# Attention rows turned on VectorE, values product in 32x64 tiles of the array, and scores behind an FFN quarter

## The chip, the cores and the metric

The kernel runs on one core of a Trainium2 chip, as one launch. The metric is the device time in microseconds. Before the change it is 1148.92 us, the median of three runs (1147.48 to 1149.34). The core's engines run their own queues in order and meet through semaphores: TensorE (PE, matrix products, its weight loads are listed as PEld), VectorE (DVE), ScalarE (ACT), GpSimd (POOL), and SyncE (SP), which here issues the DMA transfers.

## The reference, cut to what matters

A decoder layer on x of 32 sequences x 64 tokens x 256, all in float32: first a gated delta-rule attention over the tokens (8 heads of 128), then a cross attention with compressed keys and values, then a gated FFN with integer weights; after each, a residual sum and a layer norm. The change lies in the cross attention:

```python
kv_c = kv @ W_kvc                                   # 64 numbers a token
q_nope, q_rope = (q_c @ W_uq), rope(q_c @ W_qr)     # 16 heads
k_nope, v = (kv_c @ W_uk), (kv_c @ W_uv)
scores = (q_nope . k_nope + q_rope . rope(kv_c @ W_kr)) * scale
good = (k_ids <= seg_id) & (k_ids >= seg_id - LOOKBACK)
attn = softmax(where(good, scores, NEG))            # 64 keys of the own sequence
out = (attn @ v) @ W_o
x = layernorm(x + out)
```

The kernel multiplies the weights together ahead (`w_qn` from W_uq and W_uk, `w_uvo` from W_uv and W_o), so for one tile it computes the scores against `kE` and `kO`, the softmax, the product of the attention rows with the compressed tokens `kvtok` (64 numbers a token), and the product of that with `w_uvo`.

## The kernel before

There are two phases. `delta_phase` computes the delta-rule attention in 32 units over slots. `tile_phase` takes its output in 16 tiles of 128 tokens (two sequences each) through output projection, cross attention and FFN. Some tile work is done ahead, in the last slots of the first phase: `out` of tiles 0, 1, 2, rope and nope of tiles 0 and 1, the scores and the softmax of tile 0.

The tile phase is a software pipeline. Step s of each engine's `loop` (s from 2 to 19) works on tile u1 = s (output projection, norm 0, rope and nope queries), u2 = s-1 (scores, softmax), u3 = s-2 (values product, cross result, norm 1), u4 = s-3 (FFN) and u5 = s-4 (norm 2, store). The order inside a step is written out by hand for each engine, and each engine goes through it in order. On TensorE (L1797 to L1867) it is: `out(u1)` 8 products, `scores(u2)` 32 products, two transposes of x2 (L1812), eight transposes of the attention rows (L1818), `turn_x1(u1)`, `ffn(0)`, `down_q`, `ffn(1)`, `rope`, `nope`, the values product (L1841), `ffn(2)`, `ffn(3)`, the cross product (L1854) and the down product (L1866). Each float32 product appears in the trace as two instructions (two passes), a transpose as one.

The scores of a tile lie as rows (h2, query) x columns (pair of heads, sequence, key) in `att`: `score_bank(u)[b]` holds sequence b, its partitions 0 to 63 are the queries for the even head of a pair and 64 to 127 those for the odd one. TensorE transposes these rows in eight 128x128 blocks into two PSUM banks, ScalarE copies them to `attT` (L1932), and the values product takes, for each sequence b and head half h2, a 64x64 piece of the array: weights `kvtok` of the sequence (64 tokens x 64), moving 512 columns (8 head pairs x 64 queries), output in bank b1 or b2. ScalarE copies that to `ctxT` (L1942).

On VectorE (L2064 to L2099) a step is: norm 2 of u5, norm 0 of u1, `mask_scores` and `softmax_max` of u2, `hidden(0)` and `hidden(1)` of u4, `rope_parts(u1)`, in steps 2 and 3 the unpacking of `w_up` and `w_down`, `hidden(2)`, `hidden(3)`, `softmax_sum(u2)`, norm 1 of u3, `good_keys(u1)`, which builds the mask of a tile. ScalarE's step (L1907 to L1952) holds the copies out of PSUM, the silu of the FFN quarters, the exp of the softmax and the norms' Ln and Exp, with two table loads a step.

SP loads `kvtok` once, in slot U+3 of the first phase (L422, a straight 512 KB copy of the scratch). After the last slot it loads tile 3's inputs (`load(3)`) and runs `weights_after_chain` (L424), which waits until the first phase has left the region "chain" and loads `w_uvo`, the integers of `w_up` and those of `w_down`. In each step `rope_rows` (L1690) issues 16 small transfers that put the rotated q into `qE` and `qO`, which the scores of the next step need.

## Time and profile before

| | |
|---|---|
| median of three runs | 1148.92 us |
| the profiled execution | span 1150.4 us |
| TensorE busy | 1101.5 us, 96% |
| its weight loads | 763.6 us, 66% |
| VectorE busy | 818.0 us, 71% |
| ScalarE busy | 707.8 us, 62% |
| GpSimd busy | 472.0 us, 41% |
| steps 4 to 15 of the tile phase | 782.15 to 1096.67 us |

How to read it: the span is that of the one execution that the profiler took. Busy times are over the whole span, in which the first phase takes some two thirds; the change lies in the last third, so its stages are to be read by themselves. A matmul's duration in the trace is longer than the distance to the next one, since they are pipelined: what an instruction costs TensorE is the distance from its start to the start of what follows.

### The profile page before, as it was taken

What the parts mean: (1) busy time and instruction counts of PE and PEld (TensorE: products, weight loads), DVE (VectorE), ACT (ScalarE), POOL (GpSimd) and SP (SyncE); (2) the same over time, 40 slices, a digit from 0 to 9 for tenths busy, and PEclk for the clock granted to TensorE, in tenths of its full rate; (3) what the DMA queues carried; (4) which work ended last, traced back from release to release, by engine and by line L of the source; (5) the groups of instructions that cost most, each with busy time, mean ns of one, the idle gap of its engine ahead of it and who ended that gap; (6) DMA issues with size and microseconds to landing.
All of it is one profiled execution on the core that took longest, in us unless ns stands there. A gap on an engine that the chain in (4) does not pass through costs nothing.

```text
span 1150.4 us, 28703 instructions
## 1 busy us (share of the span) xinstructions
PE 1101.5 (96%) x11420; PEld 763.6 (66%) x11420; DVE 818.0 (71%) x1429; ACT 707.8 (62%) x1243; POOL 472.0 (41%) x688
## 2 busy tenths in 40 slices
PE   8989799999999999999998899899999999999998
PEld 3444455555555555655554566679998999989987
DVE  5989769879779779779776756665666665655562
ACT  5777577687786777778676666554444444444433
POOL 1649484683882873964856512310000000110000
PEclk9999899999999999999998899999999999999999
DMA  4223345656565665666646332432222211112100
GB/s 131 56 63 88 86 73 86 132 106 101 126 94 110 124 115 96 133 138 143 141 88 219 103 121 66 134 95 51 51 53 67 51 48 47 47 48 50 29 19 10
DMA packets 164213, 101.82 MB, mean 89 GB/s; under 512 B 94289, under 2 KB 144593, under 8 KB 163185
## 3 DMA queue, kind: packets, MB, share of 16 engines
q1 hardware_dynamic: 162928, 99.78, 39.2%
q8 instruction: 91, 1.49, 0.6%
q14 instruction: 42, 0.34, 0.1%
q10 hardware_dynamic: 1152, 0.21, 0.1%
HBM read 62.72 MB, written 14.67 MB: 67 GB/s over the span
## 4 chain that ended last, share of the span: by engine, by line
PE 60%; DVE 12%; POOL 10%; issue 8%; ACT 4%; SPq 3%; DMA 3%; ACTq 0%; POOLq 0%; DVEq 0%
PE proj L581 13%; PE out L1792 5%; DVE conv L1213 5%; PE turned_v_chain L1792 5%; PE proj L1854 4%; PE turned_v_chain L1866 4%; PE proj L1731 4%; POOL inverse L1490 3%; POOL rank_one L1487 3%; PE gram L596 3%; PE gram L1766 2%; PE proj L1780 1%; PE turned_v_chain L587 1%; PE proj L1841 1%; PE out L605 1%
## 5 line engine op out<-in xcount | busy, mean ns | idle before, releaser
L1213 DVE SCALAR_TENSOR_TENSOR conv<-proj,kq_weights,conv 128x504 f32<-128x504 f32 (+2 forms) x261 | 189.7, 729 | 66.3 <-ACT conv L920 60.6
L581 PE MATMUL proj<-xT,vg_weights 128*128 128x512 f32 x384 | 194.1, 629 | 3.5 <-DMA vg_weights<-in_vg_w 2.2
L2109 POOL TENSOR_TENSOR rope<-rope_part,rope_part 128x512 f32<-128x512 f32 x32 | 42.1, 1336 | 321.5 <-DVE rope_part L2040 321.5
L581 PE MATMUL proj<-xT,kq_weights 128*128 128x512 f32 x348 | 167.7, 607 | 1.3 <-DVE conv L1213 1.0
L1213 DVE SCALAR_TENSOR_TENSOR conv<-proj,vg_weights,conv 128x504 f32<-128x504 f32 (+2 forms) x192 | 139.6, 728 | 26.4 <-ACT conv L920 23.3
L1490 POOL TENSOR_TENSOR inverse<-inverse,rank_one 128x30 f32<-128x30 f32 (+14 forms) x240 | 134.5, 560 | 18.8
L1487 POOL TENSOR_TENSOR rank_one<-inverse 128x30 f32<-128x30 f32 (+14 forms) x240 | 118.1, 492 | 22.9 <-DVE inverse L1274 8.0
L581 PEld LDWEIGHTS proj<-xT,kq_weights 128*128 128x128 f32 x348 | 62.4, 190 | 76.5 <-issue 64.0
L581 PEld LDWEIGHTS proj<-xT,vg_weights 128*128 128x128 f32 x384 | 66.9, 193 | 57.9 <-issue 50.0
L596 PEld LDWEIGHTS gram<-keys_q 128*64 128x64 f32 x896 | 56.8, 136 | 42.5 <-issue 24.9
L920 ACT ACTIVATE conv<-proj,kq_weights 128x512 f32<-128x512 f32 x87 | 59.6, 685 | 40.7 <-PE proj L581 40.3
L1875 ACT ACTIVATE rstd<-rstd 128x1 f32<-128x1 f32 x48 | 9.7, 202 | 121.8 <-DVE rstd L1987 121.8
L931 ACT ACTIVATE keys_q<-conv 128x512 f32<-128x512 f32 x96 | 63.5, 664 | 27.6 <-DVE conv L1213 26.9
L596 PE MATMUL gram<-keys_q 128*64 128x128 f32 (+2 forms) x896 | 73.4, 293 | 0.6 <-DVE kq_decayed L1244 0.6
L920 ACT ACTIVATE conv<-proj,vg_weights 128x512 f32<-128x512 f32 x64 | 43.9, 685 | 27.6 <-PE proj L581 27.3
L1854 PE MATMUL proj<-t_w_uvo,ctxT 128*128 128x256 f32 x256 | 58.0, 379 | 1.3 <-issue 1.3
L1587 POOL TENSOR_TENSOR W_scaled<-W,k_norm 128x512 f32<-128x512 f32 x32 | 34.9, 1090 | 57.6 <-ACT W L1040 57.6
L1866 PE MATMUL turned_v_chain<-t_w_down,hid 128*128 128x256 f32 x256 | 57.9, 379 | 0.0
L931 ACT ACT_TABLE_LOAD x41 | 52.6, 1283 | 6.2 <-DVE conv L1213 5.5
L1866 PEld LDWEIGHTS turned_v_chain<-t_w_down,hid 128*128 128x128 f32 x256 | 48.6, 190 | 6.6
L1596 POOL TENSOR_TENSOR o_sum<-o_sum,q_sq 128x512 f32<-128x512 f32 x23 | 29.4, 1279 | 57.2 <-ACT o_sum L1143 57.2
L1854 PEld LDWEIGHTS proj<-t_w_uvo,ctxT 128*128 128x128 f32 x256 | 47.4, 190 | 7.9 <-issue 2.1
(274 smaller groups left out, 2390.3 us busy)
## 6 DMA issues: line engine op xcount, KB each, us to landing
kq_weights<-in_kq_w SPq DMA_DIRECT2D x32, 390.0 KB, 6.5
vg_weights<-in_vg_w SPq DMA_DIRECT2D x32, 390.0 KB, 6.8
o_scratch<-oT SPq DMA_DIRECT2D x32, 256.0 KB, 2.2
o_in<-o_scratch SPq DMA_DIRECT2D x16, 512.0 KB, 4.1
o_rs<-o_rs_quarters SPq DMA_DIRECT2D x88, 64.0 KB, 6.1
diagonal<-gram_decayed SPq DMA_DIRECT2D x128, 32.0 KB, 2.0
inverse<-inverse SPq DMA_DIRECT2D x32, 128.0 KB, 2.8
q_first<-rope SPq DMA_DIRECT2D x128, 32.0 KB, 1.9
```

What stands on the lines that cost most here:

```text
L581: mm = e.matmul(bank(c, u)[:], w[:, (k * 3 + c % 3) * 128:(k * 3 + c % 3 + 1) * 128], xT[g][:, k, :], start=(k == 0), stop=(k == KD - 1))
L596: mm = e.matmul(out[p, b % 4, cols], kq[:, b, S:][:, p], kq[:, b, cols], start=True, stop=True)
L920: e.activation(acc(c, u)[:], bank(c, u)[:].rearrange("p (b l) -> p b l", l=S), ACT.Copy, scale=weights(c, u)[:, j:j + 1]).then_inc(s_tap[c ...
L931: e.activation(out, acc(c, u)[:], ACT.Silu).then_inc(s_silu[c], 1)
L1213: e.scalar_tensor_tensor(acc(c, u)[:, :, back:], src[:, :, 0:S - back], weights(c, u)[:, j:j + 1], acc(c, u)[:, :, back:], ALU.mult, ALU.a ...
L1487: e.tensor_tensor(product, X[:, k + 1:, k:k + 1].broadcast_to([128, n, k]), X[:, k:k + 1, 0:k].broadcast_to([128, n, k]), ALU.mult).then_i ...
L1490: e.tensor_tensor(X[:, k + 1:, 0:k], X[:, k + 1:, 0:k], product, ALU.add).then_inc(s_elim, 1)
L1731: mm = e.matmul(out_bank(u)[:, 0:D], o_in[u % 2][:, h, :], w_out[:, h, :], start=(h == 0), stop=(h == H - 1))
L1792: mm = e.matmul(ffn_bank[r][:, (2 * i + j) * TILE:(2 * i + j + 1) * TILE], wt[:, k, (2 * r + j) * 128:(2 * r + j + 1) * 128], x2T[:, k, :] ...
L1854: mm = e.matmul(b0[:, 0:D], ctxT[:, hp].rearrange("p b q -> p (b q)"), w_uvo[:, hp, :], start=(hp == 0), stop=(hp == XH // 2 - 1))
L1866: mm = e.matmul(b6[:, 0:D], hid[:, k, :], w_down[:, k, :], start=(k == 0), stop=(k == FJ - 1))
L2109: e.tensor_tensor(turned[half][:].rearrange("p b r q -> p r b q"), parts[2 * half][:], parts[2 * half + 1][:], op).then_inc(s_turned, 1)
```

## The change

Four things change together.

1. The attention rows are laid out as (sequence, query) x (head, key): `att` is [128, 16, 64], `score_bank(u)[half]` holds eight heads, and partitions 0 to 63 are sequence 0, 64 to 127 sequence 1. The mask becomes one row of 64 keys for each partition ([128, 64] instead of [128, 2, 64]), and `seg` has a column for each tile.
2. TensorE's eight transposes and ScalarE's two copies are gone. Instead VectorE does one `transpose` of the 128x1024 attention rows (`turn_att`), which turns each 32x32 block in its place, at the end of its step, for the tile whose softmax it has just finished. `turn_att(0)` stands ahead of the loop.
3. The values product (`mix`) works with 32 keys at a time: for key half k, partition group i of 32 and head parity h2, 16 products in 32x64 tiles of the array, 256 columns each, into four banks (one for each i). Its weights `kvtok` are laid out anew, 32 partitions x (tile, key half, 64), twice the size. They are loaded in `weights_after_chain`, by four transfers, ahead of `w_uvo`. ScalarE copies the four banks to `ctxT`.
4. The order of the steps changes. TensorE: `out(u1)`, x2 transposes, `mix(u3)`, `ffn(0)`, `scores(u2)`, `turn_x1`, `ffn(1)`, `down_q`, `ffn(2)`, `rope`, `nope`, `ffn(3)`, cross, down. VectorE: norms 2 and 0, `hidden(0)`, `mask_scores`, `softmax_max`, `hidden(1)`, unpacking, `hidden(2)`, `rope_parts`, `good_keys`, `hidden(3)`, `softmax_sum`, norm 1, `turn_att(u2)`. ScalarE: x2T copy, norm 2, the ctx copies, norm 0, silu 0, x1 copy, silu 1, q copy, silu 2, the nope copies, silu 3, table, exp, norm 1.

The core of the diff:

```diff
                 def weights_after_chain():
                     e.wait_ge(s_proj[G], U)
+                    for i in range(4):
+                        e.dma_start(tiles["kvtok"][32 * i:32 * i + 32],
+                                    scratch["kvtok"][64 * (i // 2):64 * (i // 2) + 64].rearrange("(k p) n c -> p n k c", p=32)).then_inc(d_kvtok, 16)
                     e.dma_start(tiles["w_uvo"][:], scratch["w_uvo"]).then_inc(d_uvo, 16)
...
+        mix_bank = (b1, b2, b3, b4)
+        turned_att = attT[:].rearrange("p (h c) (k q) -> p h c k q", c=2, k=2)
...
                 def scores(u):
-                    wait(e, s_ctx, 2 * (u - 1))
-                    for b in range(2):
-                        for hp in range(XH // 2):
-                            q, k = (qE, kE) if hp < 4 else (qO, kO)
-                            for h2 in range(2):
-                                mm = e.matmul(score_bank(u)[b][64 * h2:64 * h2 + 64, hp * S:(hp + 1) * S], q[:, b, 2 * hp % 8 + h2, :],
+                    wait(e, s_mask, 2 * u)
+                    wait(e, s_ctx, 4 * u - 2)
+                    for half, (q, k) in enumerate(((qE, kE), (qO, kO))):
+                        for h in range(XH // 2):
+                            for b in range(2):
+                                mm = e.matmul(score_bank(u)[half][64 * b:64 * b + 64, h * S:(h + 1) * S], q[:, b, h, :],
                                               k[:, u * TILE + b * S:u * TILE + (b + 1) * S], start=True, stop=True)
...
+                def mix(u):
+                    if u == 0:
+                        e.wait_ge(done["kvtok"], 64)
+                    e.wait_ge(s_attT, u + 1)
+                    wait(e, s_nopeout, 4 * (u + 2) if live(u + 1) else 0)
+                    wait(e, s_mask, 2 * (u + 1))
+                    wait(e, s_ctx, 4 * u)
+                    for k in range(2):
+                        for i in range(4):
+                            row = slice(32 * i, 32 * i + 32)
+                            for h2 in range(2):
+                                mm = e.matmul(mix_bank[i][64 * h2:64 * h2 + 64, 0:256], kvtok[row, u, k, :],
+                                              turned_att[row, :, h2, k, :], start=(k == 0), stop=(k == 1))
+                    mm.then_inc(s_mix, 1)
...
-                            for hp in range(XH // 2):
-                                mm = e.transpose((b3, b4)[hp // 4][:, (hp % 4) * 128:(hp % 4 + 1) * 128],
-                                                 att[u3 % 2][:, hp].rearrange("p b k -> p (b k)"), ident[:])
-                            mm.then_inc(s_attT, 1)
...
+                            for i, bk in enumerate(mix_bank):
+                                e.activation(ctxT[:, :, i // 2, i % 2 * 32:(i % 2 + 1) * 32],
+                                             bk[:, 0:256].rearrange("p (h q) -> p h q", h=XH // 2), ACT.Copy).then_inc(s_ctx, 1)
...
+                def turn_att(u):
+                    if u == 0:
+                        e.wait_ge(done["scaled"], U)
+                    e.wait_ge(s_soft, 5 * (u + 1))
+                    wait(e, s_mix, u)
+                    e.transpose(attT[:].rearrange("p h k -> p (h k)"), att[u % 2][:].rearrange("p h k -> p (h k)")).then_inc(s_attT, 1)
```

## Rows read from the trace of the kernel before

**Rows 1.** The page, granted TensorE clock and busy digits in 40 slices

```profile
PE   8989799999999999999998899899999999999998
...
PEclk9999899999999999999998899999999999999999
```

**Rows 2.** Windows: busy us of PE, PEld, DVE, ACT, POOL; granted clock, DMA

```profile
900.00:950.00 50.00, 50.00 (x444) 44.96 (x444) 31.24 (x67) 23.08 (x47) 5.00 (x4) 1.00 0.22 54
```

**Rows 3.** Timeline of TensorE, one step: start, us, engine, line, operation, operands

```profile
913.20 3.62 PE L1731 MATMUL proj<-t_w_out,o_in 128*128 128x256 f32 x16
916.75 0.69 PE L1780 MATMUL proj<-t_kE,q_first 128*64 128x64 f32 x16
...
918.76 0.44 PE L1812 MATMUL turned_v_chain<-ident,x 128*128 128x128 f32 x2
919.04 1.04 PE L1818 MATMUL gram<-ident,att 128*128 128x128 f32 x8
919.91 0.38 PE L1740 MATMUL turned_v_chain<-ident,x 128*128 128x128 f32 x2
...
925.93 1.95 PE L1766 MATMUL gram<-qc,t_w_qn 96*128 96x128 f32 x16
927.81 0.65 PE L1841 MATMUL proj<-attT,kvtok 64*64 64x512 f32 x2
...
928.29 0.60 PE L1841 MATMUL proj<-attT,kvtok 64*64 64x512 f32 x2
...
928.83 1.16 PE L1792 MATMUL out<-x2T,t_w_gate 128*128 128x128 f32 x8
...
932.50 3.62 PE L1854 MATMUL proj<-t_w_uvo,ctxT 128*128 128x256 f32 x16
...
939.41 0.81 PE L1731 MATMUL proj<-t_w_out,o_in 128*128 128x256 f32 x3
```

**Rows 4.** Timeline of ScalarE and VectorE, around the softmax of a step

```profile
906.49 0.38 ACT L1904 ACTIVATE gact<-turned_v_chain 128x256 f32<-128x256 f32 x1 [0.96 <-PE turned_v_chain L1792]
...
908.19 1.06 ACT L1899 ACTIVATE att<-att 128x1024 f32<-128x1024 f32 x1
909.27 1.22 DVE L2029 TENSOR_REDUCE total<-att 128x16 f32<-128x1024 f32 x1 [1.95 <-ACT att L1899]
...
911.96 0.42 DVE L1980 TENSOR_TENSOR res<-proj,x 128x256 f32<-128x256 f32 x1
...
914.07 0.29 DVE L1969 TENSOR_TENSOR mask<-t_keys,seg 128x128 f32<-128x128 f32 x1
...
930.38 0.60 ACT L1942 ACTIVATE ctxT<-proj 128x512 f32<-128x512 f32 x1
```

**Rows 5.** Groups by line and form, VectorE: busy us, mean ns, idle before

```profile
L1287 DVE STREAM_TRANSPOSE inverse<-inverse 128x1024 f32<-128x1024 f32 x8 | 16.7, 2092 | 2.1 <-POOL inverse L1570 2.0
L1291 DVE STREAM_TRANSPOSE inverse_turned<-inverse 128x1024 f32<-128x1024 f32 x8 | 15.5, 1942 | 0.0
```

**Rows 6.** Start of the phase: timeline, and DMA issues (KB, us to landing)

```profile
739.91 0.32 SPq L429 DMA_DIRECT2D t_w_uvo<-w_uvo_scratch  x1
...
t_w_uvo<-w_uvo_scratch SPq DMA_DIRECT2D x1, 1024.0 KB, 6.3
...
t_w_qn<-w_qn_scratch SPq DMA_DIRECT2D x2, 192.0 KB, 3.5
...
744.60 0.68 DVE L2015 SCALAR_TENSOR_TENSOR att<-proj,mask 128x512 f32<-128x512 f32 x1
...
748.80 2.36 DVE L2055 SCALAR_TENSOR_TENSOR t_w_up<-w_up_ints,w_up_scale 128x1024 f32<-128x1024 int32 x2 [0.41 <-DMA w_up_ints<-in_up_w]
...
782.15 3.62 PE L1731 MATMUL proj<-t_w_out,o_in 128*128 128x256 f32 x16
```

**Rows 7.** Timeline of TensorE at the end of the phase

```profile
1093.22 3.62 PE L1866 MATMUL turned_v_chain<-t_w_down,hid 128*128 128x256 f32 x16
1098.42 0.69 PE L1780 MATMUL proj<-t_kE,q_first 128*64 128x64 f32 x16 [1.58 <-DMA q_second<-rope]
...
1134.29 0.38 PE L1812 MATMUL turned_v_chain<-ident,x 128*128 128x128 f32 x2
```

More of the change, by code:

```diff
@@ L225, in delta_phase @@
         tiles["w_uvo"] = room.again("chain", "t_w_uvo", [128, XH // 2, D])
+        tiles["kvtok"] = room.again("chain", "kvtok", [128, NT, 2, KVC])
         tiles["x_in"] = [room.again("prepare", f"x_in{i}", [128, D]) for i in range(2)]
-        tiles["kvtok"] = room.again("prepare", "kvtok", [128, NT, KVC])
         scales = {n: room.again(region, f"{n}_scale", [128, k]) for n, k, region in (
@@ L421, in first_tiles @@
                         e.dma_start(tiles["x_in"][i][:], a["x"][i * TILE:(i + 1) * TILE, :]).then_inc(d_first, 16)
-                    e.dma_start(tiles["kvtok"][:], scratch["kvtok"]).then_inc(d_w, 16)
                 def weights_after_chain():
@@ L1616, in delta_phase @@
     tiles["ints"], tiles["scales"] = ints, scales
-    done = {"o": s_og, "w_high": s_whiout, "scaled": s_gr, "stored": d_out, "weights": d_w, "first": d_first, "uvo": d_uvo, "ffn": s_wgt, "up": d_up, "down": d_down, "scales": d_gate,
+    done = {"o": s_og, "w_high": s_whiout, "scaled": s_gr, "stored": d_out, "weights": d_w, "kvtok": d_kvtok, "first": d_first, "uvo": d_uvo, "ffn": s_wgt, "up": d_up, "down": d_down, "scales": d_gate,
             "gram": s_gm, "gate": s_silu[G], "v1": s_conv[V1], "high": s_wlo, "low": s_wloout, "solve": s_solve}
@@ L1634, in tile_phase @@
         place = (early, t, t)
-        seg, below = early("seg", [128, B]), early("below", [128, 2, S])
-        mask = [early(f"mask{i}", [128, 2, S]) for i in range(2)]
+        seg, below = early("seg", [128, NT]), early("below", [128, S])
+        mask = [early(f"mask{i}", [128, S]) for i in range(2)]
         x1 = [early(f"x1_{i}", [128, D]) for i in range(3)]
@@ L1827, in loop @@
                             ffn(0, u4)
+                        if live(u2):
+                            scores(u2)
+                        if live(u1) and u1 > AHEAD:
+                            turn_x1(u1)
+                        if live(u4):
+                            ffn(1, u4)
                         if live(u1) and u1 > AHEAD:
@@ L1830, in loop @@
                         if live(u4):
-                            ffn(1, u4)
+                            ffn(2, u4)
                         if live(u1):
@@ L1835, in loop @@
                             nope(u1)
-                        if live(u3):
-                            e.wait_ge(s_attout, 2 * (u3 + 1))
-                            wait(e, s_mask, 2 * (u3 + 2) if live(u3 + 1) else 0)
-                            for b in range(2):
-                                for h2 in range(2):
-                                    mm = e.matmul((b1, b2)[b][64 * h2:64 * h2 + 64, :], kvtok[64 * b:64 * b + 64, u3, :],
-                                                  attT[64 * b:64 * b + 64, :, h2, :], start=True, stop=True)
-                            mm.then_inc(s_mix, 1)
                         if live(u4):
-                            ffn(2, u4)
                             ffn(3, u4)
@@ L1917, in loop @@
                             e.activation(x2T[:], b5[:, 0:KD * TILE].rearrange("p (k n) -> p k n", k=KD), ACT.Copy).then_inc(s_x2tout, 1)
-                        if live(u5) and not live(u1):
+                        if live(u5):
                             rsqrt(2, u5)
+                        if live(u3):
+                            e.wait_ge(s_mix, u3 + 1)
+                            wait(e, s_cross, u3)
+                            for i, bk in enumerate(mix_bank):
+                                e.activation(ctxT[:, :, i // 2, i % 2 * 32:(i % 2 + 1) * 32],
+                                             bk[:, 0:256].rearrange("p (h q) -> p h q", h=XH // 2), ACT.Copy).then_inc(s_ctx, 1)
+                        if live(u1) and u1 > AHEAD:
+                            rsqrt(0, u1)
+                        if live(u4):
+                            silu(0, u4)
                         if live(u1) and u1 > AHEAD:
@@ L2065, in loop @@
                     e.wait_ge(done["o"], U)
+                    turn_att(0)
                     for s in span:
@@ L2073, in loop @@
                             normalize(0, u1)
+                        if live(u4):
+                            hidden(0, u4)
                         if live(u2):
@@ L2077, in loop @@
                         if live(u4):
-                            hidden(0, u4)
                             hidden(1, u4)
-                        if live(u1) and u1 > AHEAD:
-                            rope_parts(u1)
                         if s == AHEAD:
@@ L2087, in loop @@
                             hidden(2, u4)
+                        if live(u1) and u1 > AHEAD:
+                            rope_parts(u1)
+                        if live(u1):
+                            good_keys(u1)
+                        if live(u4):
                             hidden(3, u4)
```

81 lines of the change are left out of this document (25 added, 56 removed).

## The prediction

> **What bounds the kernel now.** I read the page first. TensorE's busy digits are 8 and 9 all through the span and its granted clock is full in the second part [rows 1]. The change touches only the tile phase, so I then took the windows of that phase: from 900 to 950 us TensorE is busy 50.00 of 50 us at clock 1.00, VectorE 31.24, ScalarE 23.08 [rows 2]. There each tile costs what TensorE's instructions cost, and anything taken off its queue is gained, as long as no other chain gets longer than TensorE's own turn. Third, the timeline of one step gives that turn: first `out` at 913.20, next at 939.41, so 26.21 us [rows 3]. Fourth, the same timeline on ScalarE and VectorE gives the one chain that the change lengthens [rows 4]. The edges of the phase, where TensorE does wait, I read last [rows 6, 7].
>
> **TensorE's queue.** Removed: eight transposes of the attention rows, 919.04 to 919.91 = 0.87 us a tile [rows 3]. Scores move behind an FFN quarter and keep their 32 products; only the pairing changes (the two columns of the array now hold two sequences instead of two heads). The number of changes between 128x128 and smaller tiles of the array stays: mix and scores each still stand between full-size work. The x1 transposes move but cost the same.
> The values product changes from 4 matmuls of 64x64 with 512 columns to 16 of 32x64 with 256 columns. Before, all four ran at once: the first passes start at 927.81, the second at 928.29, and the next FFN quarter at 928.83, so 1.02 us in all, of which 2 x 0.48 is streaming [rows 3]. A pass of 256 columns is half as long, each of the eight tiles has four of them: 4 x 0.24 = 0.96, plus the same ending, about 1.02 again, if all eight tiles run at once. No row shows eight, or a tile of 32 rows next to three others. Bounds: below, the streaming can't shrink (each tile streams as many columns as before), so 0.96; above, if the row groups took turns (only the two column halves together), 4 x 0.96 = 3.8 us. I take 1.05, because the four-tile rows start within 0.01 us of each other with the same feeding of rows by partition and, as now, one bank for each row group.
> So a turn is 26.21 - 0.87 + 0.03 = 25.37 us.
>
> **VectorE's and ScalarE's queues.** Added: one stream transpose of 128x1024 a tile. The rows nearest are the two of the same size in the first phase, 1942 and 2092 ns [rows 5]; their access is strided, the new one's isn't. The 1942 row reads straight and writes strided; I take 1.95. Below, it can't beat the 1.22 us that the plain 1024-element operations take [rows 4]. ScalarE loses two 512-column copies and has the two ctx copies cut in four. Neither engine is full [rows 2], so only order counts. What is queued behind the new wait: `turn_att` is last in VectorE's step, behind the norm of the cross result, and `sums(2)` and `sums(0)` of the next step stand behind it; TensorE waits for it in `mix`.
> The chain starts at nope's end on TensorE, which comes a turn less one FFN quarter (half of 3.67) and cross and down (6.91) after `out` starts, at 16.65 [rows 3]. Four q copies, 2.57 (927.81 to 930.38); silu and table load 1.70 (906.49 to 908.19); exp 1.08; softmax sum, reciprocal, product 2.69 (909.27 to 911.96); the norm 2.11 (911.96 to 914.07); the transpose 1.95 and 0.05 to hand over [rows 4, 5]. Sum 12.15, so the turned rows are there at 28.8, which is 3.45 in the next step, and 3.6 with some 0.1 for hand-overs that these rows don't show. TensorE reaches `mix` after `out` with the change of tiles (3.55) and two transposes (0.28 at most), at 3.8 [rows 3]. So the transpose is hidden, with 0.2 us of cover; without that cover each further us costs one us in every step. SP's 16 row copies for the rotated q start from rope's end, which is nope's start, 13.5 before a step ends (925.93 to 939.41); where the scores waited for them, they came at 1098.42, 1.75 into the step, 15.2 after rope [rows 3, 7]. Now nope starts 10.6 before the step ends and the scores 6.8 into the next, 17.4 apart, so these copies stay hidden. The masks are half as wide (they start at 914.07 [rows 4]), hidden like before.
>
> **The start of the phase** (steps 2 and 3). kvtok was loaded long before and was free. Now it is loaded twice as large (1 MB) in pieces of 256 bytes, after the last wait of the first phase, ahead of w_uvo, w_up and w_down, and `mix(0)` with scores(1) and everything behind it waits for it. Its first issue takes w_uvo's place at 739.91. If it were as fast as w_uvo (6.3 us) it would land at 746.2; by the other 256-byte load, 384 KB in two issues 0.6 apart with 3.5 to landing (4.1 us, of which I count 1.9 as fixed, an estimate), 1 MB moves in 5.9 and with w_uvo's queueing lands near 750 [rows 6]. I take 747.4. w_uvo, w_up and w_down land some 4 us later, still ahead of their use. Then: mix(0) to 748.4; scores(1) wait for two ctx copies, from 749.4 to 751.4; mask and maximum 3.8 (744.60 to 748.39) to 755.4; unpacking w_up 2.36 to 757.8; masks 0.8 (an estimate: four operations of at most 0.29, overlapping [rows 4]); the norm 2.2 to 760.8; softmax sum 2.7 to 763.5; the transpose to 765.5 [rows 6]. From `mix(1)` the rest of step 3 takes a turn less 3.8: `out(4)` starts at 787.1 instead of 782.15 [rows 6]. **Loss: 4.95 us.**
>
> **The steady steps** 4 to 15: 12 x (26.21 - 25.37) = **10.1 us gained.**
>
> **The end.** Step 16 begins where the last full product of step 15 ends, 1093.22 + 3.45 = 1096.67; before, x2 of the last tile was turned at 1134.29, 37.6 later [rows 7]. New: `mix(14)` still waits for the chain, at 3.6, though no `out` fills the time; ffn(0) (with its first product 1.9) and the scores (2.0 and the change of tiles) end at 8.6 [rows 3]; mask and maximum to 12.6; `hidden(1)`, which VectorE now does behind them, to 13.1, and ffn(3) waits for it; silu and table 16.8; exp 17.9; sum 20.6; norm 22.7; the transpose 24.7. Then mix(15) and two FFN quarters, while VectorE and ScalarE do the delayed norm up to its scalar step (1.8 of the 2.11), four ctx copies (1.3, an estimate: cut in four, 0.5 to 0.6 each uncut before), table and silu 1.7, hidden 0.4 (as the 0.42 of the sum at 911.96), to 29.9 [rows 4]; two quarters 3.6, cross and down 6.9: 40.4. **Loss: 2.8 us.** What follows is as before.
>
> **Sum**: +4.95 - 10.1 + 2.8 = -2.3 us. On the profiled execution, 1150.4 to 1148.1. The median shown is 1.5 us below it; the same difference gives 1148.9 - 2.3 = **1146.6 us**.
>
> **The rivals.**
> A. *VectorE's transpose is as fast as its other 1024-element work*, 1.22 instead of 1.95, because it reads and writes straight. For: both rows of 2 us are strided. Against: the one with a straight read is hardly shorter. The steady step gains nothing (it is hidden), the start 0.7, the end twice 0.7 and the wait behind it, 1.8 in all: 1144.1. The Trainium skill (Vector Engine (DVE) Microarchitecture Reference, The reshape front-end and per-opcode configuration) says that the 32x32 transpose sustains one element per cycle and lane. By that rule this rival is the case; the 1942 and 2092 ns rows do not agree with it [rows 5].
> B. *The 32-row tiles don't all run together.* If four of eight do, mix is 2 x 0.96 + 0.1 = 2.0, 1.0 more in 16 tiles, and it lies on both TensorE's turn and the start's and end's chains: +15, 1162. The sign turns at 1.05 + 2.3/16 = 1.2 us for one tile's product. For: no row has it. Against: the four-tile rows lose nothing. The Trainium skill (TensorE: Matmul & The Clock Gate, Packing small matmuls) gives 3.07 of 4 for four row groups and 10.6 of 16 for sixteen tiles; an estimate at 70% of eight, with 32 passes of 0.216 (sixteen in 3.46 [rows 3]), is 6.9 / 5.6 = 1.2 us, where the change would be worth nothing; the trace has no such packing.
> C. *The chain on VectorE becomes the bound.* Its cover is 0.2 us. With the 2092 ns transpose and 0.1 more on two of the hand-overs, each of 12 steps waits 0.15, and start and end lose 0.2 to 0.4: 1149.
> D. *kvtok lands late*, near 750 or beyond because each issue writes 32 partitions only. Everything behind mix(0) moves by that: +2.6 to +4: 1149 to 1151.
>
> **How the numbers follow.** 0.2% of this kernel is 2.3 us, about what a measurement can tell from no change. The forecast has 0.38, its own range 1144.5 to 1148.5, half on each side of that bound (0.20 faster, 0.18 same). A 0.20, faster. B 0.18, slower. C 0.14: 0.10 same, 0.04 slower. D 0.10: 0.04 same, 0.06 slower. Together faster 0.40, same 0.32, slower 0.28. The range leaves out B's far part and reaches over A and D: 1142.5 to 1154.
>
> **What would show it.** Steady steps: `out` to `out` 25.4, TensorE without idle time before `mix`; if TensorE waits there for VectorE's transpose, C. The duration of the transpose decides A. The time from mix's first matmul to the next FFN quarter decides B. In the start: the landing of kvtok, and out(4) at 787. At the end: 40.4 us from step 16 to the last x2 transpose, with waits before mix(14), ffn(3) and mix(15). Wrong would be above all a steady turn that isn't 0.8 us shorter.

## The result and the profile after

| | before | after |
|---|---|---|
| median | 1148.19 us (1145.31 to 1150.19) | 1151.13 us (1149.09 to 1154.68) |
| ratio to before, 95% interval | 1 | 1.0027 (1.0017 to 1.0036) |
| profiled execution, span | 1150.4 us | 1146.9 us |

The kernel is 3.1 us slower (0.27% of 1148), where I forecast 2.3 us faster; the time lies inside the range of 1142.5 to 1154. The two spans have the opposite order of the two medians, so they mustn't be subtracted. An execution takes 2.2 us more than its span (1149.09 for 1146.9), so the span of 1150.4 belongs to an execution some 4 us slower than its kernel's median. In the second traces (e11, e12 below) the spans are 1144.7 and 1149.6. I therefore count every trace from a mark ahead of everything that the change touches in the tile phase: the first product of `rope(2)`.

The page of after: busy digits and granted clock of TensorE in 40 slices, to be held against [rows 1].

```profile
PE   8989899999999999999988899689999999999988
...
PEclk9999799999999999999999999989999999999999
```

The 26th slice (717 to 745 us) has a 6 where before has an 8. Windows of after (us; busy PE, PEld, DVE, ACT, POOL; granted clock; DMA share and GB/s), the second to be read beside [rows 2]:

```profile
700.00:750.00 50.00, 37.10 (x488) 26.50 (x488) 28.00 (x47) 23.15 (x43) 12.87 (x9) 0.92 0.44 120
900.00:950.00 50.00, 50.00 (x491) 45.56 (x490) 35.38 (x71) 21.76 (x48) 5.01 (x4) 1.00 0.21 54
```

In the middle TensorE is as full as before. At the start it idles 13 of 50 us. The timeline of TensorE in one steady step of after (start, us, engine, line, operation, operands):

```profile
914.28 3.64 PE L1733 MATMUL proj<-t_w_out,o_in 128*128 128x256 f32 x16
917.76 0.38 PE L1827 MATMUL turned_v_chain<-ident,x 128*128 128x128 f32 x2
918.07 0.43 PE L1810 MATMUL proj<-attT,kvtok 32*64 32x256 f32 x2
918.08 0.43 PE L1810 MATMUL decays<-attT,kvtok 32*64 32x256 f32 x2
918.10 0.45 PE L1810 MATMUL gram<-attT,kvtok 32*64 32x256 f32 x4
918.34 0.38 PE L1810 MATMUL proj<-attT,kvtok 32*64 32x256 f32 x2
...
919.12 1.16 PE L1794 MATMUL out<-x2T,t_w_gate 128*128 128x128 f32 x8
...
939.67 1.71 PE L1733 MATMUL proj<-t_w_out,o_in 128*128 128x256 f32 x7
```

From `out` to `out` 25.39 us, where [rows 3] have 26.21. The mix takes 1.05 us (918.07 to 919.12); its eight tiles start within 0.03 us of each other. There is no wait ahead of it. VectorE's transposes, by line and form (busy us, mean ns, idle before), beside [rows 5], and the one of this step:

```profile
L2033 DVE STREAM_TRANSPOSE attT<-att 128x1024 f32<-128x1024 f32 x16 | 19.8, 1238 | 0.0
L1289 DVE STREAM_TRANSPOSE inverse<-inverse 128x1024 f32<-128x1024 f32 x8 | 16.8, 2105 | 2.1 <-POOL inverse L1572 2.0
L1293 DVE STREAM_TRANSPOSE inverse_turned<-inverse 128x1024 f32<-128x1024 f32 x8 | 15.7, 1961 | 0.0
```

```profile
915.83 1.24 DVE L2033 STREAM_TRANSPOSE attT<-att 128x1024 f32<-128x1024 f32 x1
```

The same operation on as many elements takes 1238 ns read and written straight and 1961 or 2105 ns with strides. It ends at 917.07, 1.00 us ahead of the mix. Now the start of the phase in after: timeline of TensorE and of SP's queue (SPq), to be held against [rows 6].

```profile
735.38 1.16 PE L1759 MATMUL turned_v_chain<-qc,t_w_qr 96*128 96x128 f32 x8 [0.36 <-ACT qc L1892]
736.75 5.37 SPq L429 DMA_DIRECT2D kvtok<-kvtok_scratch  x4
742.16 1.22 SPq L431 DMA_DIRECT2D t_w_uvo<-w_uvo_scratch  x1
746.33 0.69 PE L1810 MATMUL proj<-attT,kvtok 32*64 32x256 f32 x2 [8.90 <-DMA kvtok<-kvtok_scratch]
...
749.25 1.98 PE L1782 MATMUL proj<-t_kE,q_first 128*64 128x64 f32 x32 [0.90 <-ACT ctxT L1925]
750.98 1.67 PE L1782 MATMUL decays<-t_kO,q_second 128*64 128x64 f32 x32
752.59 2.05 PE L1768 MATMUL gram<-qc,t_w_qn 96*128 96x128 f32 x16
...
787.30 3.65 PE L1733 MATMUL proj<-t_w_out,o_in 128*128 128x256 f32 x16
```

The same stretch in the chain of waits that ended last (start, us, what):

```profile
736.75 0.57 SPq L429
737.36 0.70 SPq L429
738.11 2.81 SPq L429
740.96 5.33 DMA kvtok<-kvtok_scratch
746.33 0.69 PE proj L1810 x2
...
756.41 2.35 DVE t_w_up L2055 x2
```

SP needs 5.37 us to issue the four pieces of kvtok. The fourth issue begins at 740.96, 4.21 us behind the first, and lands 5.33 us after it began. TensorE, whose queue has `mix(0)` next, stands still for 8.90 us. Behind the wait the products go at half speed: scores(1) take 3.3 us (749.25 to 752.59) where a steady step has 2.0. The granted clock of that stretch is 0.55, so for most of it TensorE has the lower of its two clock levels, 1.2 instead of 2.4 GHz (windows of after, columns as above):

```profile
745.00:753.00 8.00, 5.76 (x99) 4.61 (x100) 0.31 (x1) 1.21 (x4) 0.00 (x0) 0.55 1.01 379
```

The end, beside [rows 7]:

```profile
1093.74 0.44 PE L1827 MATMUL turned_v_chain<-ident,x 128*128 128x128 f32 x2 [1.53 <-DVE x L2001]
1094.89 0.43 PE L1810 MATMUL proj<-attT,kvtok 32*64 32x256 f32 x2 [0.72 <-DVE attT L2033]
...
1130.68 0.38 PE L1827 MATMUL turned_v_chain<-ident,x 128*128 128x128 f32 x2
```

Counted from rope(2), in us, with the second traces beside the first ones:

| stretch | before | before (e11) | after | after (e12) |
|---|---|---|---|---|
| rope(2) to out(4) | 42.05 | 42.05 | 51.92 | 52.20 |
| out(4) to the down product of step 15 | 311.06 | 311.06 | 301.29 | 301.30 |
| from there to the end of the span | 57.23 | 57.45 | 58.26 | 59.85 |
| rope(2) to the end | 410.34 | 410.56 | 411.47 | 413.35 |

So the change costs 9.9 to 10.1 us at the start, gains 9.8 in the steady steps and costs 1.0 to 2.4 at the end: +1.1 in the first trace of after, +2.8 in the second, against +3.1 measured by the ratio.

### The profile page after: what moved, and what is told of

Its sections match the earlier page's. It is cut to its first block, busy times and chain, and to the rows that moved or that the text cites. A ratio compares the mean times of both kernels' runs of the same rounds, so it can differ in the third digit from the quotient of the medians.

```text
span 1146.9 us, 29249 instructions
## 1 busy us (share of the span) xinstructions
PE 1086.5 (95%) x11676; PEld 754.1 (66%) x11676; DVE 847.6 (74%) x1445; ACT 693.9 (61%) x1243; POOL 471.7 (41%) x688
## 4 chain that ended last, share of the span: by engine, by line
PE 59%; DVE 14%; POOL 10%; issue 7%; ACT 4%; DMA 3%; SPq 3%; ACTq 0%; DVEq 0%; POOLq 0%
PE proj L583 13%; DVE conv L1215 5%; PE out L1794 5%; PE turned_v_chain L1794 5%; PE turned_v_chain L1871 4%; PE proj L1859 4%; PE proj L1733 4%; POOL inverse L1492 3%; PE gram L598 3%; POOL rank_one L1489 3%; PE gram L1768 2%; PE proj L1782 1%; DMA vg_weights<-in_vg_w 1%; PE turned_v_chain L589 1%; PE proj L1810 1%
## 5 line engine op out<-in xcount | busy, mean ns | idle before, releaser
L1733 PE MATMUL proj<-t_w_out,o_in 128*128 128x256 f32 x224 | 51.1, 381 | 1.9 <-issue 1.9
```

The costliest lines, as they stand in the source:

```text
L1733: mm = e.matmul(out_bank(u)[:, 0:D], o_in[u % 2][:, h, :], w_out[:, h, :], start=(h == 0), stop=(h == H - 1))
```

## The experiments

Theory W: the steady gain is real, and the start eats it, because mix(0) holds TensorE's queue for a load that is issued last and cut small, with the clock falling behind the wait. Rival O: the new order itself costs it, since scores(1) and everything that hangs on mask(1) now stand behind mix(0) and its copies. Rivals for a part of it: the cut of the load rather than its place, the clock, and VectorE's chain in the steady step. Each ratio is to executions of before taken alongside, whose medians lie between 1147.4 and 1149.3 us, so kernels are compared by their ratios rather than by their medians. e1 to e7 have 12 executions each, e8 has 5, e9 and e10 have 6. The last two columns come from one trace each.

| kernel | median | ratio (95%) | rope(2) to out(4) | rope(2) to end |
|---|---|---|---|---|
| after | 1151.13 | 1.0027 (1.0017 to 1.0036) | 51.92 | 411.5 |
| e1 kvtok early | 1144.96 | 0.9973 (0.9961 to 0.9985) | 46.70 | 406.3 |
| e2 busy wait | 1150.21 | 1.0027 (1.0016 to 1.0038) | 51.66 | 412.9 |
| e3 before, kvtok late | 1148.14 | 1.001 (0.9998 to 1.0021) | 43.22 | 411.6 |
| e4 mix(0) last | 1148.72 | 1.001 (0.9998 to 1.0021) | 48.82 | 410.0 |
| e5 both | 1145.07 | 0.9973 (0.996 to 0.9986) | 45.60 | 405.2 |
| e6 both, scores(15) first | 1148.81 | 1.0006 (0.9992 to 1.002) | 45.45 | 411.1 |
| e7 straight load | 1149.51 | 1.0018 (1.0004 to 1.0032) | 49.75 | 410.9 |
| e8 turned twice | 1161.95 | 1.012 (1.0099 to 1.0141) | 55.11 | 424.0 |
| e9 both, sum first | 1141.63 | 0.993 (0.9913 to 0.9947) | 43.84 | 405.0 |
| e10 as e9, end reordered | 1142.69 | 0.9946 (0.9927 to 0.9966) | 44.71 | 404.8 |

**e1, kvtok with the first tiles.** It takes the sbuf place of w_up's scale, which moves behind w_uvo.

```diff
     def first_tiles():
+        for i in range(4):
+            e.dma_start(tiles["kvtok"][32 * i:32 * i + 32], ...)
     def weights_after_chain():
-        for i in range(4):
-            e.dma_start(tiles["kvtok"][32 * i:32 * i + 32], ...)
         e.dma_start(tiles["w_uvo"][:], ...)
+        e.dma_start(scales["w_up"][:], a["up_scale"])
```

> The kernel after, with the four kvtok transfers issued with the first tiles' loads instead of behind the whole chain of the first phase (kvtok takes the place of w_up's scale in the sbuf, and that scale is loaded behind w_uvo). Everything is computed. Theory W (the late, finely cut kvtok load holds TensorE's queue): attT(0) ends at 741.10 in the trace of after, 3.7 us behind rope(2)'s end at 737.4, so the wait ahead of mix(0) falls from 8.90 to about 3.7 us and turns into one on VectorE; the halved clock behind it (mix(0) passes 0.43 instead of 0.21 us, scores(1) 3.3 instead of 2.0) goes too or gets shorter. 5.2 to 7.5 us less than after: 1143.6 to 1146 us, some 2 to 4.5 below before. Theory O (the new order costs at the start: scores(1) stands behind mix(0) and its four ScalarE copies, and everything later hangs on mask(1) and the chain behind it, whatever kvtok does): at most 2 us less than after, 1149 to 1151, not below before.

Theory W is borne out: 1144.96 us, and out(4) 5.2 us earlier. The load is gone from TensorE's waits (timeline of e1; its rope(2) began at 737.91):

```profile
743.73 0.69 PE L1811 MATMUL proj<-attT,kvtok 32*64 32x256 f32 x2 [3.77 <-issue]
...
746.64 1.97 PE L1783 MATMUL proj<-t_kE,q_first 128*64 128x64 f32 x32 [0.90 <-ACT ctxT L1926]
```

3.77 us are left, until attT(0) is there, and the clock still falls (0.54 from 743 to 750). This one edit turns the loss of 0.27% into a gain of 0.27%.

**e2, TensorE busy while it waits.**

```diff
 def mix(u):
+    if u == 0:
+        for _ in range(18):
+            e.matmul(b1[:, 0:256], ident[:], kE[:, 0:256], start=True, stop=True)
     if u == 0: e.wait_ge(done["kvtok"], 64)
```

(Not in this excerpt: mix's waits for banks and masks are moved ahead of the 18 products.)

> The kernel after, with 18 matmuls of 256 columns (identity by kE, into a bank that scores(1) overwrites) in front of the kvtok wait of mix(0), some 7.7 us at full clock: the wait stays, TensorE is busy through most of it. Everything of the kernel is computed. Theory W with the clock as its second part: kvtok still lands at about 746.3, but the granted clock does not fall behind it, so mix(0) takes 1.05 instead of about 1.9 us and scores(1) 2.0 instead of 3.3: about 2.2 us less than after, 1149 us. Rival (the half clock has no part in the loss, or the clock falls in any case): within 0.5 us of after, 1151.

By the ratio, nothing is gained. The trace shows a gain at the place itself that is lost later: nope(2) begins 15.2 us after rope(2) instead of 17.2, so 2.0 us are saved by full clock; then the first FFN quarter of step 3 runs at half speed, behind two waits of 1.9 us each, where after had full speed. The clock granted behind the wait is 1.00 here, against the 0.55 of after (window of e2):

```profile
745.00:750.00 5.00, 3.37 (x98) 2.81 (x99) 0.12 (x1) 1.21 (x4) 0.00 (x0) 1.00 1.02 403
```

```profile
745.73 0.43 PE L1812 MATMUL proj<-attT,kvtok 32*64 32x256 f32 x2 [1.35 <-DMA kvtok<-kvtok_scratch]
...
762.99 0.43 PE L1812 MATMUL proj<-attT,kvtok 32*64 32x256 f32 x2 [1.87 <-DVE attT L2035]
...
764.04 2.08 PE L1794 MATMUL out<-x2T,t_w_gate 128*128 128x128 f32 x8
```

In this trace the price of the clock was taken in another place, and by the ratio it could not be mended by itself.

**e3, the kernel before with its straight kvtok load at the late place.**

```diff
 def weights_after_chain():
+    e.dma_start(tiles["kvtok"][:], scratch["kvtok"])
     e.dma_start(tiles["w_uvo"][:], ...)
```

> The kernel before, its kvtok load left in one straight piece of 512 KB but moved to where the kernel after has it: behind the chain of the first phase, ahead of w_uvo. Everything is computed. If a late load by itself is harmless and the harm lies in the cut (four issues of 1024 short rows each, 5.37 us of SyncE and 5.3 to 6.9 us to land): one straight issue of some 0.4 us lands by about 743 to 745, at or before the time when the mix(0) of before comes up (its scores(1) are masked at 744.6), and the time is that of before within 1 us, 1148 us. If the place in the queue does the harm (kvtok's own landing, or w_uvo, w_up and w_down half a megabyte later): 3 us or more slower than before, 1151 or above.

One straight issue of 512 KB takes SP 0.32 us and lands in 5.2 us, at 741.5, and the mix of before comes up at 743.03 and doesn't wait. Only w_up's unpacking starts 2.4 us later, counted from rope(2), than in e11, and out(4) comes 1.2 us later: 1.001. So this load at the late place is nearly harmless for the old order: 1.2 us in the trace, and a ratio that can't be told from 1. It is half as large as after's and uncut, though. The mix of before comes up 8.3 us behind rope(2), and after's load lands 10.95 us behind it; from these two an estimate for the old order with after's load is a wait of 2.6 us. No run had it.

```profile
736.34 0.32 SPq L428 DMA_DIRECT2D kvtok<-kvtok_scratch  x1
...
750.87 3.69 PE L1731 MATMUL proj<-t_w_out,o_in 128*128 128x256 f32 x16 [1.80 <-issue]
```

**e4, the first mix behind scores(1) and nope(2).**

```diff
 if live(u3):
+    if u3 == 0:
+        scores(u2)
+        nope(u1)
     mix(u3)
```

> The kernel after, with only the first mix behind scores(1) and nope(2) in its step (and the ScalarE copies of mix(0) behind those of nope(2)); all other steps keep the order of the change. Everything is computed. Theory W (it is a block of TensorE's queue by a late load): the 3.8 us of scores(1) and nope(2) fill part of the 8.9 us wait, mask(1) comes at about 741 instead of 752.7, mix(0) still waits to 746.3, for about 5 us. From there the step has 3.8 us less to do, and scores(1) does not run at half clock: 4 to 6 us less than after, 1145 to 1147 us. Theory O agrees in sign, since the order is mended: it expects the whole 9.9 us of the start back, 1141 us, as the chain behind mask(1) is then 11.7 us earlier. Rival (loss in the steady steps or the end): no difference, 1151.

1148.7 us: about half of what theory W expected, a quarter of what O did. The wait is still 5.62 us, and now the cross product stands in the slow stretch (clock 0.61 from 746 to 757) and takes 5.86 us instead of 3.62:

```profile
746.77 0.69 PE L1810 MATMUL proj<-attT,kvtok 32*64 32x256 f32 x2 [5.62 <-DMA kvtok<-kvtok_scratch]
...
750.20 5.86 PE L1862 MATMUL proj<-t_w_uvo,ctxT 128*128 128x256 f32 x16 [1.42 <-issue]
```

**e5, both mends together.**

> The two mends together: the kernel after with kvtok loaded with the first tiles and, in its first step only, mix(0) behind scores(1) and nope(2). Everything is computed. Measured from the start of rope(2), out(4) came at 42.0 us in the trace of before, 51.9 in after, 46.7 with kvtok early, 48.8 with mix(0) last. In the last of these mix(0) still waited 5.6 us for kvtok, and mix(0) and the cross product ran at half clock for 3.2 us more. If the start's loss is this wait and the clock behind it, both go and out(4) comes at about 40 to 43 us, the median at 1139 to 1142 us, 6 to 9 below before (ratio 0.992 to 0.995). If the two mends get hold of the same microseconds (VectorE's chain with w_up's unpacking then sets attT(1)), out(4) stays at 45 to 46 and the time at 1144 to 1145, that of kvtok early.

By the numbers it is the second of the two cases: out(4) at 45.6, the time that of e1. The two mends get hold of the same microseconds. The reason is another than the expectation's, w_up's unpacking: the cross product runs at half speed here too, 6.43 us instead of 3.62, and VectorE waits for it ahead of softmax_sum(1), which e9 takes up. With kvtok there, mix(0) waits for something new: ScalarE's four copies of nope(2), whose banks it needs, and mix(1) waits for attT(1) as in after.

```profile
744.39 0.43 PE L1811 MATMUL proj<-attT,kvtok 32*64 32x256 f32 x2 [2.73 <-ACT q_second L1903]
...
746.92 6.43 PE L1863 MATMUL proj<-t_w_uvo,ctxT 128*128 128x256 f32 x16 [1.40 <-issue]
...
759.60 0.43 PE L1811 MATMUL proj<-attT,kvtok 32*64 32x256 f32 x2 [1.78 <-DVE attT L2039]
```

**e6, besides scores(15) at the head of step 16.**

```diff
+if u2 == NT - 1: scores(u2)
 (x2 transposes, ffn(0, u4))
+if u2 == NT - 1: mix(u3)
```

(Not in this excerpt: ScalarE's silu(0) of that step goes ahead of the ctx copies, and VectorE's mask(15) to the head of its step.)

> As the kernel with both mends, and besides in the first step without an output projection (step 16 of the tile phase) scores(15) ahead of the x2 transposes, mix(14) behind the first FFN quarter, ScalarE's silu(0) ahead of the copies of ctx and VectorE's mask(15) at the head of its step. Everything is computed. In after, the waits of that step and the next are 1.53 us for x2, 0.72 for attT(14), 0.47 for hid, 0.85 for x2 and 0.71 for attT(15). If these are what the new order costs at the end, scores(15) covers the first two and an earlier mask(15) the last: 1.5 to 3 us less than the kernel with both mends. If they are only moved (mix(14) waiting for mask(15), cross for the later copies): within 0.5 us of it.

Refuted, 3.7 us slower than e5. At the head of its step scores(15) waits for the last row copies of the rotated queries, 4.93 us, and half clock follows (its 32 products take 3.6 us instead of 2.0). Without `out` nothing else covers the copies, which the change's later place of the scores does. Since mix(14), silu(0) and mask(15) moved with them, how much of the 3.7 us is the scores' is not shown apart; the wait is 4.93.

```profile
1091.72 1.98 PE L1783 MATMUL proj<-t_kE,q_first 128*64 128x64 f32 x32 [4.93 <-DMA q_second<-rope]
```

**e7, the load straight, at the late place.** The scratch is written in the order of the tile (eight small stores for each of four large ones), and one issue reads 128 rows of 8 KB.

```diff
 def weights_after_chain():
-    for i in range(4):
-        e.dma_start(tiles["kvtok"][32 * i:32 * i + 32], scratch["kvtok"][...].rearrange("(k p) n c -> p n k c", p=32))
+    e.dma_start(tiles["kvtok"][:], scratch["kvtok"])
```

> The kernel after, its kvtok load at the same place but straight: the stores of the first phase write the scratch in the order of the tile (eight pieces for each of four, in place of one), and one issue reads 128 rows of 8 KB, the same 1 MB. Everything is computed. Theory C (the cut of the load is what is late: 5.37 us of issues on SyncE and the last piece landing 6.9 us after its own): one issue lands 6.3 us later, as w_uvo's 1 MB does, at about 743 where after has 746.3: the wait at mix(0) falls from 8.9 to about 5.5 us and w_uvo comes 5 us sooner; 3 to 4 us less than after, 1147 to 1148 us, level with before. Theory S (it is the size and the place): the wait stays over 8 us and the time within 1 us of after. The longer stores could cost something in the first phase; the start of rope(2) in the trace would show that.

The same 1 MB lands 7.0 us after its issue began, instead of 9.6; the wait falls from 8.90 to 6.44 us, and out(4) comes 2.2 us sooner. The ratio is 1.0018, 1 us below that of after with overlapping intervals, short of the 3 to 4 us expected (theory C had the wait at 5.5). So by the trace the cut has about a quarter of the start's 9.9 us; moving the load (e1) gives back 5.2.

```profile
744.74 0.69 PE L1811 MATMUL proj<-attT,kvtok 32*64 32x256 f32 x2 [6.44 <-DMA kvtok<-kvtok_scratch]
```

**e8, each tile's rows turned twice on VectorE.**

```diff
+e.transpose(attT, att[u % 2]).then_inc(s_twice, 1)
+e.wait_ge(s_twice, u + 1)
 e.transpose(attT, att[u % 2]).then_inc(s_attT, 1)
```

> The kernel after with VectorE turning each tile's attention rows twice, the second after the first. Everything is computed. In the steady step of after, attT is ready at 917.07 and TensorE comes to the mix at 918.04: 0.97 us of cover. A second transposition of 1.24 us with its hand-over moves attT by 1.3 us. If TensorE sets the step and this cover is all there is, each of the 12 steady steps gets 0.3 to 0.4 us longer (a wait on attT ahead of each mix, step 25.7 us) and the waits at start and end some 1.3 us each, 3 times: 8 us more than after, 1159 us. If VectorE's chain were already the bound of the step, the whole 1.3 us would show in each: 16 us and more, 1169 or above. If the cover is larger than the trace shows: within 3 us of after.

The steady step becomes 25.73 us (917.40 to 943.13), +0.34, with a wait of 0.26 ahead of the mix: of 1.25 us more on VectorE, 0.9 to 1.0 were hidden. The cover of 1.00 us that the trace shows is the cover there is, and TensorE sets the step. Of the 12.5 us that the trace has more than after's, 4.1 are these steps; the rest lies where there was no cover, 3.2 at the start and 5.3 from step 15's down product on, half clock there included, for which the expectation had too little (8 us in all).

```profile
917.40 3.64 PE L1733 MATMUL proj<-t_w_out,o_in 128*128 128x256 f32 x16
...
920.23 1.25 DVE L2035 STREAM_TRANSPOSE attT<-att 128x1024 f32<-128x1024 f32 x1
...
921.53 0.43 PE L1810 MATMUL proj<-attT,kvtok 32*64 32x256 f32 x2 [0.26 <-DVE attT L2035]
```

**e9, e5 with softmax_sum(1) at its usual place.**

```diff
-if live(u2) and u3 != 0: softmax_sum(u2)
+if live(u2): softmax_sum(u2)
 (sums(1, u3), normalize(1, u3))
-if u3 == 0: softmax_sum(u2)
```

> The kernel with both mends, and VectorE's softmax_sum(1) in the first step at the place that it has in all others, ahead of the residual sums of x2 instead of behind them. Everything is computed. In the trace of both mends exp(1) ends at 749.19 and VectorE then idles 3.18 us for the cross product, does the sums, and only then softmax_sum(1) and turn_att(1); mix(1) waits 1.78 us for attT(1). If that wait stands on the path to out(4), it goes: 1.5 to 1.8 us less than both mends, 1143.4 us, ratio to before 0.996. If something else takes its place (x2T, the fourth bank, SyncE's rope rows), within 0.5 us of both mends, 1145.

The wait of mix(1) is gone (its products start at 757.46 behind the x2 transposes, without one), and out(4) comes 1.76 us sooner than in e5. This is the version that beats both kernels: 1141.63 us, ratio 0.993 (0.9913 to 0.9947), some 8 us faster than before. More than the 0.996 expected, and clear of e5's interval (0.996 to 0.9986). In its trace half clock stood in step 16 as well, so that rope(2) to the end is only 0.2 us less than in e5. The cross product of its first step still takes 6.53 us instead of 3.62, at a clock of 0.56.

**e10, e9 with the last two steps rearranged** (x2's sums ahead of softmax_sum from step 15 on, mix(14) and mix(15) behind the first FFN quarter).

> The kernel of the run before it, and the last two steps rearranged: from step 15 on VectorE does the sums of x2 ahead of softmax_sum, and in steps 16 and 17 mix stands behind the first FFN quarter. Everything is computed. In after these two steps wait 1.53 and 0.85 us for x2 and 0.72 and 0.71 for attT, and both waits stand ahead of the first FFN quarter. If this is what the new order costs at the end, x2 comes before it is asked for and the FFN quarter covers attT: 2 to 3.5 us less than the kernel without it, 1140 to 1141.5 us, ratio 0.994, and less of the half clock that was seen near 1093 in four of the runs. If the waits only move (scores(15) for the copies of mix(14)): within 0.7 us of it. The earlier try at the end waited 4.93 us for the rope rows of step 15, which SyncE delivers at 0.6 us a piece; here scores(15) is not moved ahead.

Nothing gained, 0.9946 with overlapping intervals: the waits move. For x2 and attT TensorE no longer waits, but for these (waits of e10: us in total, times, longest):

```profile
PE out L1795 <- DVE hid L2056: 1.8, 1, 1.8
PE out L1795 <- ACT x2T L1925: 1.4, 3, 0.5
...
PE proj L1783 <- ACT ctxT L1934: 1.2, 1, 1.2
```

**e11 and e12, before and after once more, unchanged.**

> The kernel before, unchanged, for a second trace. In its first trace rope(2) began at 740.11 with the clock at half for 10.2, 6.8 and 3.4 us in the stretch from 600 to 740; in all nine traces of its variants and of after it began between 733.2 and 737.9. If that trace was a late one for reasons of the first phase only, this one has rope(2) at about 735 and the same 410.3 us from there to the end of the span (to within 0.5), so that the comparison of the tile phases stands: after is 1.1 us longer there. If the tile phase of before itself differs from one execution to the next, the 410.3 will not come back.

> The kernel after, unchanged, for a second trace. Its first trace had a mean granted clock of 0.986, the highest of its 17 runs (mean 0.983), and an execution time 2.0 us below its median. Four variants of it showed the clock at half for 3.4 us near 1093, where TensorE waits for x2 and attT in the first step without an output projection. If that is what the typical execution has and the first trace lacked, this trace shows it, with 1.7 us more from rope(2) to the end: 413 instead of 411.5 us. If not, the 2 us lie in the first phase.

Both as expected: before has 410.56 us from rope(2) to the end (410.34 in its first trace) and 42.05 to out(4), to the hundredth. After has 413.35: 0.3 us more at the start, and half clock in step 16 behind the waits for x2 and attT. In e12 the FFN quarter of 2.0 us takes 3.5 there:

```profile
1094.95 0.44 PE L1827 MATMUL turned_v_chain<-ident,x 128*128 128x128 f32 x2 [1.53 <-DVE x L2001]
...
1097.18 2.08 PE L1794 MATMUL out<-x2T,t_w_gate 128*128 128x128 f32 x8
1099.05 1.74 PE L1794 MATMUL out<-x2T,t_w_up 128*128 128x128 f32 x8
```

And e11 shows what was peculiar in the first trace of before: there w_uvo was issued 0.20 us ahead of rope(2), here 1.64 us behind it. TensorE's granted clock from 735 to 740 us was 0.67 there, and `rope(2)` began 11.63 us behind `out(2)` instead of 10.26. The trace of e9 has the same (0.68 from 730 to 735), and its w_uvo was issued 0.01 us ahead of rope(2). In the other twelve traces SP's first issue of these weights came 1.1 to 2.1 us behind it.

```profile
734.12 1.16 PE L1757 MATMUL turned_v_chain<-qc,t_w_qr 96*128 96x128 f32 x8 [0.36 <-ACT qc L1887]
...
735.76 0.32 SPq L429 DMA_DIRECT2D t_w_uvo<-w_uvo_scratch  x1
```

## Why the prediction was wrong

**TensorE's turn: right.** 25.37 forecast, 25.39 measured; the mix at 1.05 as taken, so rival B is out. The twelve steps brought 9.8 us instead of 10.1.

**VectorE's transpose: rival A.** 1.24 us, not 1.95. I let the strided rows of the first phase decide [rows 5] where the unstrided 1024-element rows [rows 4] were the nearer kin. The rule of the Trainium skill that was named there (Vector Engine (DVE) Microarchitecture Reference, The reshape front-end and per-opcode configuration: one element per cycle and lane) agrees with L2033, which is as fast as a plain operation of that size, and not with L1289 and L1293, which it doesn't tell apart. The chain is ready 0.8 us earlier than in my sum (0.7 of it the transpose's), the cover is 1.0 us instead of 0.2, and rival C is out (e8).

**The start: the step that failed.** 4.95 us of loss forecast, 9.87 in the first trace. By its terms, counted from rope(2):
- *When the load is issued.* I put it 0.20 us ahead of rope(2), from [rows 6]. It came 1.37 behind: **+1.6**. In that trace of before TensorE had half clock just ahead of rope(2), so that rope(2) was 1.4 us late against SP's queue; in e11 the same issue stands at +1.64. Two queues that don't wait for each other had been tied together by one execution.
- *How long it takes.* I took 7.5 us from the first issue to the landing (747.4 less 739.91); it was 9.6: **+2.1**. It is the cut, into four issues and short rows: e7's straight load needs 7.0. SP alone is busy 5.37 us with four issues; I had the row of two such issues 0.6 us apart and didn't carry it on to four issues of more rows.
- *The clock.* I had no term for it: **+2.0** (e2 gives it: nope(2) at 15.2 instead of 17.2; counted from the start of mix(0) it is 4.0 instead of 6.3, since e2's load landed 0.2 later). The window from 900 to 950 has clock 1.00, and I used durations at full clock behind a wait that I had forecast myself. The page of before already shows three 8s in its clock row, all of them in slices where TensorE's own row has a 7 or an 8, and two of them just past the middle of the span, where I had called the clock full [rows 1].
- *The transpose*, faster: **-0.7**.

Together 4.95 + 1.6 + 2.1 + 2.0 - 0.7 = 9.95. My sum also went from 751.4 by 3.8 to 755.4, 0.2 too far, and did the same at the end (8.6 to 12.6), too little to matter. Rival D (kvtok lands late, 1149 to 1151 us) had the right event, a late landing that moves everything behind mix(0), and its landing "near 750 or beyond" was right as well: 10.95 us behind rope(2) is 751.1 in the time of that trace. I gave it 0.10. Its reason, that each issue writes 32 partitions only, no run tested by itself, and that its time of 1149 to 1151 us was met is partly luck, since 1.4 of the 1.6 us by which the issue came late are TensorE's clock in one trace of before and the time holds the clock's 2.0 as well. The issue's place and the landing are 3.7 of the 5.0 us that the start was off, and the landing's part lies in choosing 747.4 nearer to the straight w_uvo than to the other load of 256-byte pieces, whose estimate was 750. The Trainium skill says of such loads (DMA: Bandwidth & Descriptors, Specifications) that below 512 bytes a piece they lose line rate; e7 against after agrees, 7.0 against 9.6 us for the same megabyte. But e7 has one issue instead of four as well, and after's fourth begins 4.21 us behind its first; no run here tells the short pieces from the time of the issues.

**The end: right in kind, too large.** From the start of step 16 to the last x2 transposes 38.6 us instead of 40.4, which is what rival A gives; the loss is 1.0 us in the first trace, not 2.8. In e12 half clock behind the waits of step 16 adds 1.6 (2.4 in all, against e11), so the typical loss is near my number for a reason that I didn't have. Half clock in this stretch showed in e2, e4, e6, e7, e8, e9 and e12, and not in after's first trace, e1, e5 and e10. What decides it in one execution stays open; it always stands behind these waits, and none of the three traces with the order of before has it.

**The sum.** Forecast +4.95 - 10.1 + 2.8 = -2.3. Measured +9.9 - 9.8 + 1.0 = +1.1 in one trace, and +10.15 - 9.76 + 2.4 = +2.8 in the other. The sign hung on a start that I took from one execution and one load. That the median was put 1.5 us below the span did no harm, since only the difference of the kernels counts: the medians differ by 2.9 us, the two pairs of traces by 1.1 and 2.8.

**What was shown and what only argued.** That the load's place and cut cost the start is shown (e1, and the trace of e7); that the new order makes the wait expensive, because mix(0) now stands first, by e4, while e3, with half the load, only agrees. Of the start's 9.9 us, 5.2 go with the load moved (e1), 1.1 more with the first mix last (e5) and 1.8 more with softmax_sum(1) in its usual place (e9). The last 1.8 are unmended; the cross product at half speed stands there, 2.9 us longer, but no run shows what would be left without it. The clock's 2.0 us are shown in the trace of e2, but e2 is no faster as a whole, so they are part of the price of waiting rather than a cost of their own. Over all timed runs the mean granted clock is 0.990 for before, 0.983 for after, 0.987 for e1 and 0.987 for e9: even the best version has more half clock than before, and its gain is what is left after that.

## What to carry to other kernels

A gain in the steady steps is multiplied by their number, but a pipeline pays it back at both ends: when an order is changed, walk through the first and the last steps with every load's issue and landing, and count the issues, since many short rows keep the issuing queue busy for microseconds. Put first in a queue only what is sure to be there; a load that was free behind 8 us of other work (the mix of before in e3) is on the path once its reader stands at the head. Take offsets between two engines that don't wait for each other from more than one execution, and give each forecast wait of TensorE a second term for the clock behind it.

## What the runs showed of the hardware

- One operation, two speeds: VectorE's 32x32 block transpose of 128x1024 float32 takes 1.24 us straight and 1.96 to 2.11 us strided.
- Sixteen matmuls in 32x64 tiles of the array, 256 columns each, take 1.05 us with one bank for each row group: eight tiles run together, 0.03 us apart, against four tiles of 64x64 at 1.02 for the same work [rows 3].
- Four issues of 256 KB in rows of 256 bytes keep SP busy for 5.37 us (0.57 to 2.81 each); one straight issue of 1 MB (e7) keeps it 0.32 us. Issued 100 us earlier, in e1, the four take 5.24 us.
- Keeping TensorE busy through one wait (e2) kept the granted clock at 1.00 behind it, against 0.55 in after, and it fell at the next waits instead (0.57 from 764 to 768).
